# A graph network of four layers on one core: the messages of layers 1 to 3 in two multiplications, each with its own signal

## The reference

```python
h = (x @ W).reshape(n, HEADS, C)
a_s = jnp.einsum('nhc,hc->nh', h, att_src)
a_d = jnp.einsum('nhc,hc->nh', h, att_dst)
e = jax.nn.leaky_relu(a_s[src] + a_d[dst], NEG_SLOPE)
m = jax.ops.segment_max(e, dst, num_segments=n)
p = jnp.exp(e - m[dst])
z = jax.ops.segment_sum(p, dst, num_segments=n)
alpha = p / (z[dst] + EPS_SOFTMAX)
msg = h[src] * alpha[:, :, None]
out = jax.ops.segment_sum(msg, dst, num_segments=n)
```

## Time and profile before

| | us |
|---|---|
| median of 3 runs | 12334.37 |
| lowest and highest | 12312.73, 12349.45 |
| the profiled execution's own time | 12336.85 |
| its span in the trace | 12335.1 |
| PE busy | 7368.8 (60%) |
| DVE busy | 5183.6 (42%) |
| POOL busy | 6252.3 (51%) |
| ACT busy | 2180.5 (18%) |

### The profile page before, as it was taken

The page is one execution under the profiler, slowest core; times in us unless marked ns, Lnnn a source line. Parts: engine busy times, 40 slices in busy tenths (PEclk is TensorE's granted clock), DMA queues, the critical chain, the costliest instruction groups (busy, mean ns, idle before and its releaser), DMA issues.

```text
span 12335.1 us, 141293 instructions
## 1 busy us (share of the span) xinstructions
PE 7368.8 (60%) x41611; PEld 6500.9 (53%) x41612; DVE 5183.6 (42%) x13628; ACT 2180.5 (18%) x7255; POOL 6252.3 (51%) x6594
## 2 busy tenths in 40 slices
PE   5666666666565555665565555555555555565554
PEld 5655555555555545554455555554544555555554
DVE  3222222224444444444464444444445444444445
ACT  2111111112111111111121111111112111111112
POOL 4555555554455545554445555555544555555553
PEclk7777777777777777777767777777776777777776
DMA  3222222222211111111122121121112221111111
GB/s 88 55 55 55 55 54 55 56 55 59 51 47 47 47 45 47 47 46 45 46 67 48 47 48 48 48 48 48 47 47 55 49 48 48 48 48 48 48 48 42
DMA packets 425594, 625.69 MB, mean 51 GB/s; under 512 B 189754, under 2 KB 305737, under 8 KB 425285
## 3 DMA queue, kind: packets, MB, share of 16 engines
q0 software_dynamic: 206336, 462.61, 15.4%
q1 hardware_dynamic: 218910, 160.84, 5.0%
q10 hardware_dynamic: 296, 1.65, 0.0%
HBM read 598.03 MB, written 26.58 MB: 51 GB/s over the span
## 4 chain that ended last, share of the span: by engine, by line
another core or an unknown queue 29%; PE 25%; DVE 23%; issue 16%; DVEq 4%; ACT 2%; POOL 1%; DMA 0%; SPq 0%; ACTq 0%; POOLq 0%
PE ps L713 12%; PE ps L760 7%; DVE acc L1263 5%; DVE memb L1183 4%; DVEq L1237 2%; PE ps L703 2%; DVE msg L1356 2%; DVE msg L1276 1%; DVEq L1263 1%; PE ps L791 1%; DVE acc L1253 1%; DVE shared L1310 1%; PE ps L795 1%; DVE shared L1348 1%
## 5 line engine op out<-in xcount | busy, mean ns | idle before, releaser
L568 POOL DMA_INDIRECT G<-rows,idx x6448 | 6112.1, 948 | 5686.5 <-DVE msg L1356 2881.2
L713 PE MATMUL ps<-msg,memb 128*128 128x136 f32 (+2 forms) x12896 | 2052.4, 328 | 62.9 <-DVE msg L1356 62.2
L760 PE MATMUL ps<-membT,shared 128*104 128x128 f32 x9672 | 2082.8, 400 | 2.2 <-ACT membT L925 2.2
L713 PEld LDWEIGHTS ps<-msg,memb 128*128 128x128 f32 x12896 | 1976.0, 236 | 84.0 <-issue 41.1
L760 PEld LDWEIGHTS ps<-membT,shared 128*104 128x104 f32 x9672 | 1874.9, 270 | 29.5 <-issue 3.0
L703 PE MATMUL ps<-ident,memb 128*128 128x128 f32 x6448 | 1108.2, 302 | 1137.5 <-issue 750.3
L1183 DVE TENSOR_TENSOR memb<-rel,ps 128x768 f32<-128x768 f32 x1488 | 1044.4, 729 | 1509.1 <-PE ps L713 1227.7
L703 PEld LDWEIGHTS ps<-ident,memb 128*128 128x128 f32 x6448 | 770.4, 150 | 1393.4 <-issue 1034.4
L925 ACT ACTIVATE membT<-ps 128x512 f32<-128x512 f32 x1984 | 991.3, 510 | 1961.8 <-remote 1639.2
L732 PE MATMUL ps<-shared,membT 128*128 x3224 | 813.8, 336 | 754.2 <-DVE msg L1276 472.5
L1263 DVE TENSOR_TENSOR acc<-acc,ps 128x136 f32 (+2 forms) x3472 | 1023.0, 295 | 561.7 <-issue 315.5
(11 more groups left out here) (182 smaller groups left out, 4864.9 us busy)
## 6 DMA issues: line engine op xcount, KB each, us to landing
G<-rows,idx POOLq DMA_INDIRECT x6448
shared<-marks_all SPq DMA_DIRECT2D x372, 156.0 KB
shared<-in_edge_attr SPq DMA_DIRECT2D x124, 256.0 KB
shared<-in_edge_attr SPq DMA_DIRECT2D x124, 160.0 KB
rows<-msg SPq DMA_DIRECT2D x36, 288.0 KB, 2.7
idx<-in_src SPq DMA_DIRECT2D x496, 6.5 KB
xrows<-msg SPq DMA_DIRECT2D x24, 256.0 KB, 2.2
memb<-xrows SPq DMA_DIRECT2D x24, 256.0 KB, 2.9
```

Of the source, the lines that this page charges most:

```text
L568: nc.gpsimd.indirect_dma_start(G[:, b, t, 0:rows[l].shape[1]], None, rows[l], bass.IndirectOffsetOnAxis(idx[:, b, t:t + 1], 0)).then_inc(g ...
L713: last = mm(ps_sum[k // 2][:, 0:width], memb[:, b, k * P:(k + 1) * P], msg[:, b, k, 0:width], start=k % 2 == 0, stop=k % 2 == 1 or k == K - 1)
L760: last = mm(ps_sc[b][0:JH, :], adz[:, k // 2, K - 1 - k:K - 1 - k + JH], membT[:, k, :], start=k == 0, stop=False)
```

## The change

The multiplication L1356 is split in two: tiles 0 to 5 (128x6x136) and tiles 6 to 12 (128x7x136), in this order and with nothing between them. Each has a semaphore of its own; the second keeps the old one, `messages`, the first has a new one, `first_messages`. POOL waits for `first_messages` of chunk c - 2 before the first gather of a chunk, and for `messages` of that chunk before the gather of tile 6. PE waits for `first_messages` before the sums, and in layers 1 to 3 for `messages` before the sum of tile 6. In layer 0 both semaphores are incremented at the same place.

```diff
     HALF = 8
+    FIRST = 6
...
         messages = chunk_sem("messages_ready")
+        first_messages = chunk_sem("messages_of_first_tiles_ready")
...
                 pool.wait_ge(idx_loaded[b], 16 * (PAIRS * l + h + 1))
                 if not early:
-                    pool.wait_ge(messages, past(l, c - 2))
+                    pool.wait_ge(first_messages, past(l, c - 2))
                 pool.sem_inc(gather_paced, 1)
                 for t in range(K):
+                    if t == FIRST and not early:
+                        pool.wait_ge(messages, past(l, c - 2))
+                        pool.sem_inc(gather_paced, 1)
                     nc.gpsimd.indirect_dma_start(
...
                 for k in range(K):
                     if l == 0 and k in (0, 4, 8, 12):
                         pe.wait_ge(hidden[k // 4], past(0, c))
+                    if l and k == FIRST:
+                        pe.wait_ge(messages, past(l, c))
...
-                pe.wait_ge(messages, past(l, c))
+                pe.wait_ge(first_messages, past(l, c))
                 if l == 1:
                     pe.wait_ge(maxf_kept, gpast(l, c))
                 sums(l, c, b, SW if l == 1 else MW, None)
...
                 dve.wait_ge(pre_added[3], past(0, c))
+                dve.sem_inc(first_messages, 1)
                 dve.sem_inc(messages, 1)
...
                 dve.wait_ge(wgt_turned, gpast(l, c))
-                tt(msg[:, b, :, 0:MW].rearrange("p k (h f) -> p k h f", h=H),
-                   G[:, b, :, 0:MW].rearrange("p k (h f) -> p k h f", h=H),
-                   ps_wgt.rearrange("p (h k) -> p k h", h=H).unsqueeze(3).to_broadcast([P, K, H, FW]),
-                   ALU.mult).then_inc(messages, 1)
+                for k0, k1, done_with in ((0, FIRST, first_messages), (FIRST, K, messages)):
+                    tt(msg[:, b, k0:k1, 0:MW].rearrange("p k (h f) -> p k h f", h=H),
+                       G[:, b, k0:k1, 0:MW].rearrange("p k (h f) -> p k h f", h=H),
+                       ps_wgt.rearrange("p (h k) -> p k h", h=H)[:, k0:k1, :].unsqueeze(3)
+                       .to_broadcast([P, k1 - k0, H, FW]), ALU.mult).then_inc(done_with, 1)
```

## The result

The changed kernel took 12575.36 us (median of 4, 12566.57 to 12602.2), the kernel before in the same comparison 12337.31 (12312.73 to 12349.45): a ratio of 1.0199, 95% interval 1.0177 to 1.0221. It is 238 us slower. The forecast of 12,395 us lies 58 us above the same kernel before: the right side, and the result is inside the range, but the forecast is a quarter of the size.

The account below looks back on a forecast made before the run. It took the first gather of a chunk to pace its own successor through POOL. Of 359 us gained, 420 to 435 are given back, a loss of 60 to 75, carried to the median: 12,395 us, range 12,030 to 12,680.

Parts of the forecast that it names:

- What bounds the kernel: Layers 1 to 3: a turn closes through POOL, the first gather pacing its own successor; L1337 starts 18.43 us after it.
- The multiplication in two: L1356 on DVE: parts of 1.00 and 1.14 us, last signal 0.15 us later; 56 us of DVE work, hidden in a wait.
- The gathers and the second wait on POOL: On POOL: first gather 0.99 us earlier, at most 359 us gained; the wait before tile 6's gather taken as costing nothing.
- the bound of 239 us: Rival that the wait before tile 6's gather breaks POOL's rhythm: up to 239 us more, 12,640 us; chance 0.05.
- The sums: On PE: no earlier start in turns where PE is busy, 0.3 to 0.4 us earlier where PE is ahead.
- What the earlier gathers do to PE: Layers 1 to 3: PE's signals get caught among gathers; 420 to 435 us given back, leaving a 60 to 75 us loss.
- The gain arrives: Rival: each turn of layers 1 to 3 0.99 us shorter, 11,975 us, or 12,100 if a third is lost; chance 0.27.
- The late turn spreads: Rival: most layer 1 turns end sums past 5 us and take 27.0 us; 12,700 to 12,730 us; chance 0.18.

Follow-up runs that it names:

- the gathers alone: Against the kernel before: multiplication split, gathers on the first and second signal, sums on the second only; 0.9999 in the short condition, 1.0253 in the long one.
- the split alone: Against the kernel before: multiplication in two parts, but gathers and sums both wait for the second signal; 8755.51 us, ratio 1.000, short condition.
- The sums alone: Against the kernel before: multiplication split, sums on the first and second signal, all gathers on the second; 0.991 in the short condition, 0.9889 in the long one.

## Why the prediction was right or wrong

- **What bounds the kernel.** Right for the condition of the first result. L1345 again starts 18.38 us after the first gather of a plain turn, and the gathers alone, with the sums on their old signal, make the kernel 2.5% longer. The first gather paces its own successor in plain turns; in the late ones L1345 stands 20.9 us after it. Wrong as a statement of the kernel alone: in the short condition POOL is bound by its own issuing.
- **The multiplication in two.** Right. The halves took 1004 and 1138 ns against 1.00 and 1.14 us, and the split alone measured 1.000 (short condition only).

```profile
L1365 DVE TENSOR_TENSOR msg<-G,ps 128x952 f32<-128x952 f32 x372 | 423.4, 1138 | 0.0
L1365 DVE TENSOR_TENSOR msg<-G,ps 128x816 f32<-128x816 f32 x372 | 373.4, 1004 | 276.9 <-PE ps L798 271.2
```

- **The gathers and the second wait on POOL.** Right in what they cost POOL. The first gather starts 1.79 us after L1365 (5925.51 to 5927.30), as worked out, and the one of tile 6 follows the last before it by 1.25 us (5910.71 to 5911.96): no rhythm is broken, the bound of 239 us stays unused.
- **The sums.** Undersized. I took up to 0.4 us in some turns. In the plain turns of layer 1 they start 1.47 us after L1365 does, at the median, where it was 2.59 us: 1.1 us earlier; in the late ones, 2.68 us after it, nothing is gained. The sums alone are worth 1.1% in the long condition. This term was a gain I had left nearly at nothing, but it is not what made the miss.
- **What the earlier gathers do to PE.** This term was mis-sized, and it is the error. The direction was right: the sums' end moved from 3.7 to a median of 4.9 us after the first gather in layer 1 (4.6 to 5.0 forecast), and L1318 from 12.1 to 18.3 us (15 to 17 forecast). The price was wrong. I gave +0.75 us to three fifths of the turns of layer 1 and together +60 us; its pauses grew by 150. In the very place for which I had worked out 25.6 − 0.99 = 24.6 us, sums that end 4.5 to 5.0 us after the gather, stand 27 turns of layer 1, and their median is 26.5 us. For layers 2 and 3 I took 0 to +15; they grew by 95. I had priced a plain turn midway between two rows, and 23.9 us, as if lengths between them were to be had. In layer 1 they aren't: a turn is 22.9 us, or the scores' own signal comes late too, L779 is issued 10.9 instead of 5.3 us after the first gather in the two turns shown, and the turn is 25.4 to 27.2 us, 27.1 at the median. The kernel before has no such second lateness: its L1294 waits for an unnamed releaser twice in the whole span, L1302 111 times in layers 1 to 3. I also held the sums' length fixed, though the earlier trace rows show it at 4.12, 3.45 and 5.43 us; it goes with the clock, as does their start.
- **The gain arrives.** Wrong for the first result, true of each plain turn, and nearly true in the short condition, by another mechanism: 1% faster through the sums. The Trainium skill, SBUF — State Buffer, "SBUF: two separate sides", by which a DMA cannot slow a compute operation and PE waits for no other user of SBUF, fits the short condition, where the gathers alone measured 0.9999. In the long one the same edit measured 1.0253. No run shows that it is SBUF where the signals are held up, so the rule isn't refuted; the 11,975 us worked out for this rival is.
- **The late turn spreads.** Nearest in mechanism. It had 0.18 and 12,700 to 12,730 us, which is 125 to 155 too high: about a third of layer 1's turns stay plain at 22.9 us, which it did not allow for, and nearly three fifths in layers 2 and 3. Its boundary at 5.0 us is too high: the 27 turns just named lie below it and are late. For the gathers alone its price holds: 106 of 107 turns, and a median of 27.3 us against the 27.0 that it gave.
- **Slips of the working.** 25.6 − 23.9 − 0.99 is 0.71 and not 0.75 us, which makes 53 instead of 56. The second signal is out some 7 us before the gather of tile 6, not 6. And a range up to 12,680 leaves out the whole of the late turn's 12,700 to 12,730, not the upper part of it. None of them changes the outcome.

**What stays open.** What holds PE's signals up, and what puts a chip into one condition or the other, no run tells; both conditions have the same instructions and a gather of 0.94 us. The ends of matmuls in the rows are modelled, so the rows don't even tell whether a signal is late or the matmuls before it are. The whole change was never met in the long condition by an experiment; its 2% stands on the first result, and on the two halves. I tried no kernel in which a wait on the gathers keeps them back until the end phase is through.

**The better version.** The sums on two signals and the gathers on the second: 0.991 in the short condition and 0.9889 in the long one. It is the only one measured faster than the kernel before in both, though in the short condition the whole change gets 0.9898.

## What to carry to other kernels

When the start of a transfer paces a loop, and the steps behind it come late while it runs, an earlier start of the transfer is not a gain to be booked at its size: look at where the steps behind it then stand, and in what turns. Read such a turn as one of a few kinds, count the kinds, and price a shift as turns that change kind, not as microseconds added to a mean. Look at the granted clock of each kind as well. A release split in two can help one consumer and harm another, so measure each consumer alone.

## What the runs showed of the hardware

- The same kernel takes 8748 to 8758 us or 12,757 to 12,862 us (12,337 in the first comparison), by a condition that changed on two chips from one time to another. The sign of the changed kernel's effect differs with it: 0.990 or 1.020.
- In the long condition DVE and ACT start up to 9.6 us after the modelled end of PE's matmuls, in the turns shown, while gathers are going out, with no releaser in the trace: L1318 3.4 us after L779's end in the plain turn shown (5910.23 to 5913.60), 7.0 us in the late one (5938.72 to 5945.72). In the short condition no such wait was seen in layer 1. Ends that stand ahead of the eight transposes on PE are read 1.2 us after their end, behind them 8.4 us, at the same distance from the first gather (6.5 to 8.5 us).
- 26 matmuls of 128x144 took 3.45 us at a granted clock of 1.00 and 5.23 us at 0.68.
- Fewer matmuls on PE lowered the granted clock from 0.83 to 0.75 and made the kernel 3.5% slower.
